# Edge scores of a graph layer: one-hots made before the sums on ScalarE, arrivals signalled by GpSimd, SyncE's loads and releases in order of slots

## The reference, cut to what matters

```python
for l in range(2):
    q = (x @ Wq[l] + bq[l]).reshape(N, H, D)      # H = 8 heads, D = 64
    k = (x @ Wk[l] + bk[l]).reshape(N, H, D)
    v = (x @ Wv[l] + bv[l]).reshape(N, H, D)
    a = (q[dst] * k[src]).sum(-1) / sqrt(D)       # the scores
    e = exp(a - segment_max(a, dst)[dst])
    alpha = e / (segment_sum(e, dst)[dst] + 1e-16)
    agg = segment_sum(alpha[:, :, None] * v[src], dst).reshape(N, C)
    x = agg + (x @ Ws[l] + bs[l]) + enc
```

## Time and profile before

| | us |
|---|---|
| median of 3 runs (3148.83 to 3156.06) | 3154.48 |
| the profiled execution | 3161.87 |
| its span, first to last instruction | 3160.2 |
| mean granted TensorE clock, share of full speed | 0.907 |
| VectorE busy | 2163.0 |
| TensorE busy | 2531.4 |
| GpSimd busy | 1648.5 |
| ScalarE busy | 1170.8 |

### The profile page before, as it was taken

How to read it: one execution, slowest core, us unless ns; L and a number is a source line. 1 busy time by engine, 2 the same in 40 slices (tenths; PEclk the granted TensorE clock), 3 DMA queues, 4 the chain that set the end, 5 groups by cost and what they waited for, 6 DMA issues and landing times. The chain is left out here.

```text
span 3160.2 us, 50179 instructions
## 1 busy us (share of the span) xinstructions
PE 2531.4 (80%) x9914; PEld 1849.9 (59%) x9914; DVE 2163.0 (68%) x3476; ACT 1170.8 (37%) x4350; POOL 1648.5 (52%) x1559
## 2 busy tenths in 40 slices
PE   1888787765898779977877669888785999699998
PEld 1666444443775557744544358666564767477776
DVE  5776677878977666657877888677464454566665
ACT  0554566654000021136666610001353322155554
POOL 0111677777777741146767777777122443355555
PEclk8999788986899989988888779999887999899999
DMA  2666777776777776667777767777432332251110
GB/s 96 237 239 213 246 240 242 240 236 197 204 218 220 218 236 228 197 216 238 240 242 239 221 185 214 213 224 221 150 134 93 106 121 93 98 167 41 40 46 33
DMA packets 244253, 575.14 MB, mean 182 GB/s; under 512 B 32642, under 2 KB 70894, under 8 KB 242834
## 3 DMA queue, kind: packets, MB, share of 16 engines
q0 software_dynamic: 100160, 328.28, 35.8%
q1 hardware_dynamic: 126546, 212.27, 19.7%
q10 hardware_dynamic: 17280, 31.63, 2.7%
HBM read 465.00 MB, written 107.06 MB: 181 GB/s over the span
## 5 line engine op out<-in xcount | busy, mean ns | idle before, releaser
L1357 POOL DMA_INDIRECT edge_ring<-k_rows,edges_src x626 | 592.7, 947 | 282.3 <-issue 135.9
L1357 POOL DMA_INDIRECT edge_ring<-v_rows,edges_src x626 | 617.2, 986 | 223.5 <-issue 140.6
L1666 PE MATMUL edge_psA<-layer_q_space 128*128 128x256 f32 (+1 forms) x2656 | 628.9, 392 | 95.3 <-DVE layer_q_space L1490 87.8
L1666 PEld LDWEIGHTS edge_psA<-layer_q_space 128*128 128x128 f32 x2656 | 495.5, 192 | 228.4 <-issue 159.2
L1490 DVE TENSOR_TENSOR layer_q_space<-edge_ring,edge_psQ 128x512 f32<-128x512 f32 x664 | 426.6, 683 | 162.1 <-SPq L1275 133.1
L1413 DVE TENSOR_TENSOR edge_ring<-edge_psQ,edge_ring 128x512 f32<-128x512 f32 x532 | 346.9, 682 | 175.5 <-ACT edge_ring L1502 71.6
L1502 ACT ACTIVATE edge_ring<-edge_ring 128x64 f32<-128x64 f32 x1328 | 320.1, 242 | 285.9 <-DVE edge_ring L1413 285.9
L1619 PE MATMUL edge_psQ<-layer_q_space,edge_hotT 128*128 x1064 | 363.3, 474 | 15.9 <-DVE edge_ring L1413 13.3
L108 PE MATMUL proj_psP<-proj_w,proj_xT 128*128 128x512 f32 x1440 | 354.9, 403 | 6.5 <-DVE proj_xT L866 4.0
L108 PEld LDWEIGHTS proj_psP<-proj_w,proj_xT 128*128 128x128 f32 x1440 | 270.8, 191 | 68.8 <-DVE proj_xT L866 4.4
L1394 DVE TENSOR_REDUCE layer_scores<-edge_ring 128x24 f32<-128x1536 f32 x166 | 289.1, 1742 | 0.0
(11 more groups left out here) (309 smaller groups left out, 3625.8 us busy)
## 6 DMA issues: line engine op xcount, KB each, us to landing
v_xT<-proj_xT SPq DMA_DIRECT2D x40, 512.0 KB, 4.9
edge_x_halves<-v_xT SPq DMA_DIRECT2D x80, 256.0 KB, 5.4
agg_rows<-layer_q_space ACTq DMA_DIRECT2D x40, 260.0 KB, 3.6
base_rows<-proj_enc SPq DMA_DIRECT2D x40, 256.0 KB, 2.0
k_rows<-proj_out ACTq DMA_DIRECT2D x40, 256.0 KB, 3.8
v_rows<-edge_ring ACTq DMA_DIRECT2D x40, 256.0 KB
edge_ring<-k_rows,edges_src POOLq DMA_INDIRECT x626, 4.0
edge_ring<-v_rows,edges_src POOLq DMA_INDIRECT x626, 3.8
```

Source lines behind the costliest of these rows:

```text
L1357: pool.indirect_dma_start(ring[:, buffer[n], :], None, rows, bass.IndirectOffsetOnAxis(ap=T["src"][:, t:t + 1], axis=0)).then_inc(landed[b ...
L1666: last = pe.matmul(psA[:, bass.ds(d % 2, 1), e, 0:hi - lo].rearrange("p o w -> p (o w)"), hot[:, s % R, :], wv[:, s % R, lo:hi], start=Fal ...
```

## The change

Three edits, all in `edge_attention`:

1. ScalarE: in batch j it makes the one-hot of batch j first and sums for batch j-2 after it.
2. GpSimd signals the arrivals itself: before gather n it waits for the landing of gather n-4 and signals it, then waits for the buffer's release, and gathers. The signal `started`, for which nothing waited, goes.
3. SyncE no longer waits for landings. Its releases, loads of rows and loads of x halves are sorted by a slot number: the release of tile r at r+16, the rows of block k at 8k-12, the x half h at four times the batch in which half h-3 is used up.

```diff
 (SyncE)
-                BLOCKS = -(-USED // PER_ROWS)
-                for k in range(BLOCKS):
...
-                    for h in halves_by_block.pop(k, ()):
-                        load_half(h)
-                    if k:
-                        for t in range((k - 1) * PER_ROWS, min(k * PER_ROWS, ET) if k < BLOCKS - 1 else ET):
-                            release(t + AHEAD - NB, multiplied)
-                            arrive(t, k_arrived)
...
+                def done_in(h):
+                    i, half = divmod(h, 2)
+                    return V_AT[i] + 1 + half
+                load_rows(0)
+                load_rows(1)
+                sp.wait_ge(k_arrived, K_FIRST + 1)
...
+                in_turn = [(r + 16, release, (r, multiplied)) for r in range(ET - 3)]
+                for k in range(2, -(-USED // PER_ROWS)):
+                    in_turn.append((k * PER_ROWS - 12, load_rows, (k,)))
+                for h in range(XH, 2 * NT):
+                    in_turn.append((done_in(h - XH) * B, load_half, (h,)))
+                for _slot, do, what in sorted(in_turn, key=lambda x: x[0]):
+                    do(*what)
...
-                for t in range(ET):
-                    if t + AHEAD < ET:
-                        release(t + AHEAD - NV, weighted)
-                    arrive(ET + t, v_arrived)
+                for r in range(ET - NV):
+                    release(r, weighted)
 (GpSimd)
+                def arrive(n):
+                    pool.wait_ge(*landing[n])
+                    pool.sem_inc(k_arrived if n < ET else v_arrived, 1)
                 def gather(n, rows, t):
-                    if n >= FLIGHT:
-                        pool.wait_ge(*landing[n - FLIGHT])
...
                 for t in range(ET):
+                    if t >= FLIGHT:
+                        arrive(t - FLIGHT)
                     if t >= NB:
                         pool.wait_ge(k_released, t - NB + 1)
-                        pool.sem_inc(started, 1)
                     gather(t, k_dram, t)
...
-                    pool.sem_inc(started, 1)
                     gather(n, v_dram, t)
+                for n in range(2 * ET - FLIGHT, 2 * ET):
+                    arrive(n)
 (ScalarE)
                 for j in range(BATCHES):
-                    if j >= 2:
-                        reduce(j - 2)
                     act.wait_ge(spread, j + 1)
...
                     act.activation(hotT[j % 2], apart[:, j % 2, :], ACT.Relu, bias=1.0, scale=-1.0
                                    ).then_inc(hotT_ready, 1)
+                    if j >= 2:
+                        reduce(j - 2)
```

More of the change, by code:

```diff
@@ L1196, in edge_attention @@
         PER_ROWS = 8
-        AHEAD = 6
         ring = m.sb("ring", [P, NV, C])
@@ L1251, in edge_attention @@
         rows_in = [m.sem(f"rows_in{half}") for half in range(2)]
-        started, reduced_act, lifted, topped, spread, hotT_ready, queried, multiplied, reduced, distant, padded = (
-            m.sem(x) for x in ("started", "reduced_act", "lifted", "topped", "spread", "hotT_ready", "queried", "multiplied", "reduced", "distant", "padded"))
+        reduced_act, lifted, topped, spread, hotT_ready, queried, multiplied, reduced, distant, padded = (
+            m.sem(x) for x in ("reduced_act", "lifted", "topped", "spread", "hotT_ready", "queried", "multiplied", "reduced", "distant", "padded"))
         nearby, turned, in_rows, steps, ends_done, ends_in, best_done, best_out, ready, exped, returned, stored = (
@@ L1272, in _ @@
             def _(sp):
-                def arrive(n, signal):
-                    sp.wait_ge(*landing[n])
-                    sp.sem_inc(signal, 1)
                 ends_of = {}
                 def release(r, used):
-                    if r < 0:
-                        return
                     if r // B not in ends_of:
@@ L1296, in load_half, with load_rows @@
                                      :, :, half * 2 * P:(half + 1) * 2 * P]).then_inc(half_in[h % XH], 16)
[L1298 to L1307, removed]
-                BLOCKS = -(-USED // PER_ROWS)
-                for k in range(BLOCKS):
+                def load_rows(k):
                     n = min(PER_ROWS, USED - k * PER_ROWS)
@@ L1316, in _ @@
                                  ).then_inc(rows_in[k % 2], 16)
-                    for h in halves_by_block.pop(k, ()):
-                        load_half(h)
-                    if k:
-                        for t in range((k - 1) * PER_ROWS, min(k * PER_ROWS, ET) if k < BLOCKS - 1 else ET):
-                            release(t + AHEAD - NB, multiplied)
-                            arrive(t, k_arrived)
[L1323 to L1333, removed]
+                def done_in(h):
[4 more added lines that the diff above has]
+                sp.wait_ge(k_arrived, K_FIRST + 1)
+                sp.dma_start(wv_parts.rearrange("p h k c -> p (h k c)"), later_v["w"]).then_inc(wv_in, 16)
+                sp.dma_start(bias_rows, later_v["bias"].rearrange("o (h c) -> (o h) c", h=2)).then_inc(wv_in, 16)
+                for h in range(XH):
+                    load_half(h)
+                in_turn = [(r + 16, release, (r, multiplied)) for r in range(ET - 3)]
[5 more added lines that the diff above has]
+                    do(*what)
                 sp.wait_ge(queried, USED)
@@ L1342, in _ @@
                 sp.wait_ge(stored, len(parts))
-                sp.sem_inc(v_arrived, V_FIRST - 1)
-                for t in range(ET):
-                    if t + AHEAD < ET:
-                        release(t + AHEAD - NV, weighted)
-                    arrive(ET + t, v_arrived)
+                for r in range(ET - NV):
+                    release(r, weighted)
             @block.gpsimd
@@ L1359, in gather @@
                                             ).then_inc(landed[buffer[n]], 16)
+                pool.sem_inc(k_arrived, K_FIRST - 1)
+                pool.sem_inc(v_arrived, V_FIRST - 1)
                 for t in range(ET):
+                    if t >= FLIGHT:
+                        arrive(t - FLIGHT)
                     if t >= NB:
                         pool.wait_ge(k_released, t - NB + 1)
-                        pool.sem_inc(started, 1)
                     gather(t, k_dram, t)
-                pool.wait_ge(v_stored, 16 * NT)
                 for t in range(ET):
                     n = ET + t
+                    arrive(n - FLIGHT)
+                    if t == 0:
+                        pool.wait_ge(v_stored, 16 * NT)
                     if t < NB:
```

## The result

The changed kernel took 3203.99 us (median of 4 runs, 3201.98 to 3209.97), the kernel before 3153.72 beside it: 1.0165 times as long, interval 1.0146 to 1.0183. It is 50 us slower, where 3140.5 was forecast and 3168 was the upper end of the range. The profiled execution has a span of 3208.3 us, 48.1 more than before.

The account below looks back on a forecast made before the run. GpSimd's line of gathers was taken to set the time. Of 51.4 us of waits in the scores, single loads would leave 37.4 (38 x 0.7 + 36 x 0.3); 3154.5 less 14.0 gives 3140.5 us, range 3116 to 3168.

Parts of the forecast that it names:

- What bounds the kernel: The line of 626 gathers on GpSimd sets a round's length; the score arithmetic only has to stay inside the ring.
- the landing theory of the earlier trace: With four gathers in flight, one landing later than 5.0 us stops the line; the next starts 0.30 us after it.
- (a): ScalarE's one-hots ahead of its sums: fewer waits of TensorE and VectorE, no time saved, as the gathers cover it.
- (b): GpSimd waits for and signals arrivals itself: cost between 0 and 6 us, taken as 0.
- (c): SyncE's releases and loads sorted by slot: x halves go singly, saving 14 us of gather waits in the scores.
- a pair: Two x halves loaded back to back in the scores: 1.8 us of gather waiting; a single 0.3, near a store 0.7.
- The weighting keeps its gathers, stores and scans: 0: The weighting, a round's second gather stage, was taken to change by 0 us.
- Collision of store and half (slower): Rival, chance 0.16: stores of v and x halves collide in the scores, 28 us slower, 3182 us.
- Release late after all: Rival, chance 0.12: SyncE's releases had been late and the new order mends both stages, 55 us saved, 3099.5 us.
- Bytes, not spacing: Rival, chance 0.20: loads cost the transfer engines as much singly as in pairs, no change, 3154.5 us.
- SyncE stuck: Rival, chance 0.04: SyncE held behind loads that wait for TensorE, so releases come late, 3240 us.
- The signs: One-hot waits mostly gone, last products within 12 us of the first v gather, no paired loads, scores' waits down 7 us per round.

Follow-up runs that it names:

- two_signals: The changed kernel with a second, unused signal between the arrival's signal and the gather: 3218.42 us.
- wait_on_gather: The changed kernel, but each gather itself waits for the landing four earlier, whose arrival is signalled ahead of the next gather: 3148.46 us, repeated 3144.82.
- act_only: The kernel before with ScalarE's new order alone (one-hots ahead of the sums): 3151.98 us, ratio 0.9992.
- after_old_act: The changed kernel with ScalarE's old order (sums ahead of the one-hots): 3209.85 us, ratio 1.0168 to the kernel before.
- swap_only: The kernel before with GpSimd's wait for the landing moved to the signal `started` and the release's wait to the gather: 3216.88 us.
- pairs: The kernel with landings waited for by the gather itself, its x halves loaded two at a time: 3151.10 us, beside 3144.82 with singles.

## Why the prediction was wrong

- **What bounds the kernel** held. Time follows the waits of the gathers in every run, whoever is named as the releaser, and the landing theory of the earlier trace rows is what two_signals, wait_on_gather and the runs with more in flight bear out.
- **(a), ScalarE's order, at nothing:** right (act_only, after_old_act).
- **(b), GpSimd's signals, is the step that failed:** "Upper bound: the signal now stands between a landing that was waited for and the next gather; at about 0.1 us for each of some 60 waits this is 6 us. I take 0". The place was right, the numbers were wrong. The 0.1 came from no row; it is about what one more signal costs (0.08, two_signals), and left out the gather behind the signal. A held-up gather restarts 0.53 us later; 132 gathers of the kernel before wait over 0.36, not 60 (84 in the scores alone); and as the margin shrinks to 4.23 us there are 199 of them. Against the same kernel without this wait (wait_on_gather) the edit costs 58 us of waiting (135.4 - 77.2). The reason given for 0, that the 0.30 holds in all unhindered waits, could not see this: in those the landing came long before, and they show 0.30 after the change too. The row that would have priced it was not in the trace: every landing there is waited for by the gather itself. Why a gather takes 0.75 us behind a waiting signal stays open.
- **(c), SyncE's order, 14 us:** right in its direction, though hidden, and about twice too large in time: without the cost of (b) the kernel is 0.22% and 0.24% faster than before (wait_on_gather and its repeat), 7 to 8 us. The waits in the scores, predicted to fall from 51.4 to 37.4, went from 49.8 to 36.5 and 31.2; but the execution that was traced before was itself 7 us above the median. The make-up was off: a pair costs some 0.3 us over two singles, not 1.2, while the mean of a single, 37.4 / 74 = 0.51, is about the 33.9 / 74 = 0.46 measured, if all of these waits are put down to the loads. The price of a pair had been read from one gather, the 2.10 of the earlier trace rows.
- **"The weighting keeps its gathers, stores and scans: 0"** fell with (b). The four gather stages hold 114.8 us over the step of 1.253 before and 155.1 after; of these 40.3 us the two weightings have 25.0 (27.5 to 40.4 and 28.8 to 40.9), the scores 15.3, as there the order of the loads gives something back (swap_only, with the old order, holds 84.1 us in its scores, the changed kernel 73.8). The remaining 8 us of the span's 48.1 lie between the rounds (2.3) and after the second (5.3). Over all traces here these two parts vary by 4.9 and 8.0 us, so they need no cause in the change.
- **The rivals.** None named the place of the wait. *Collision of store and half (slower)* gave the right sign for a wrong reason: wait_on_gather has the same loads and stores and is faster than before. *Release late after all* is out: in the kernel before the held-up gathers start 0.25 us behind a landing, after the change SyncE waits 112 times at its releases, and six in flight take the waits away without touching it. *Bytes, not spacing* is out by the runs of pairs, though the spacing is worth little. The sharing of the engines, for which the Trainium skill, "DMA: Bandwidth & Descriptors", section "Issuing engines are not separate DMA queues", stood beside it, agrees with the trace: a gather lands later behind a load of SyncE (6.5 us in the earlier trace rows, 3.8 in the median of the kernel before). *SyncE stuck* did not happen.
- **The signs.** Those of the edits themselves came true: TensorE's waits for one-hots at 2.9 us, the last products 7.7 us behind the first v gather, no loads in twos. That of the time did not: the waits in the scores rose, and so did those in the weighting.

## What to carry to other kernels

A wait is worth what stands behind it: on the gather that it is for, the gather started 0.25 us after the landing; on a signal ahead of it, half a microsecond later than that. So let the critical instruction carry its own wait and put the signal after it (or tell the arrival a step later). And where a pipeline waits for landings, count the steps in flight against the slowest landings first: two more gathers in flight were worth 72 us to the kernel before, more than every reordering here.

## What the runs showed of the hardware

The restart of a GpSimd gather of 256 KB: 0.25 us after the landing when it carries the wait, 0.78 behind a signal that carries it, 0.86 behind two; in both of the latter the gather starts 0.75 us behind the last signal. I had expected a difference of 0.1.

A gather begun during a scan on VectorE ends only after the scan. VectorE's first scan, and GpSimd's gather beside it, kernel after:

```profile
759.64 5.76 DVE L1419 TENSOR_TENSOR_SCAN layer_q_space<-layer_q_space 128x2688 f32<-128x2688 bf16 x1
...
760.50 5.65 POOL L1342 DMA_INDIRECT edge_ring<-v_rows,edges_src  x1 [0.30 <-DMA edge_ring<-v_rows,edges_src]
```

The gather takes 5.65 us in place of 0.95, one begun in the second scan 5.49, and each ends 0.75 us after its scan: some 9 us per round. With a few longer gathers behind them the v gathers of a round take 10 to 12 us more than 0.947 each, in every kernel here, also with six in flight. No run was made to test the cause.
